# An RWKV block with routed experts: the gated rows are turned behind the k product instead of between r and k

## What is computed

```python
h = _layernorm(x, ln1_g, ln1_b)
hp = _shift(h)
xr = tm_mu_r * h + (1.0 - tm_mu_r) * hp      # xk, xv alike
r = jax.nn.sigmoid(jnp.einsum('btc,dc->btd', xr, tm_Wr))
k = jnp.einsum('btc,dc->btd', xk, tm_Wk)
v = jnp.einsum('btc,dc->btd', xv, tm_Wv)
ek = jnp.exp(tm_u + k)
wkv = ek * v / (ek + 1e-08)
x = x + jnp.einsum('btc,dc->btd', r * wkv, tm_Wout)
```

## Time and profile before

| | |
|---|---|
| median of 3 runs | 1719.45 us (1712.07 to 1720.55) |
| profiled execution, device time | 1702.0 us |
| its span in the profile | 1700.3 us |
| PE busy | 1643.6 us (97%), 8817 matmuls |
| DVE busy | 1326.2 us (78%) |
| ACT busy | 770.3 us (45%) |
| POOL busy | 417.9 us (25%) |
| mean granted clock of TensorE | 0.993 |

### The profile page before, as it was taken

How to read it: one execution, slowest core, us unless ns; L and a number is a source line. 1 busy time by engine, 2 the same in 40 slices (tenths; PEclk the granted TensorE clock), 3 DMA queues, 4 the chain that set the end, 5 groups by cost and what they waited for, 6 DMA issues and landing times.

```text
span 1700.3 us, 26873 instructions
## 1 busy us (share of the span) xinstructions
PE 1643.6 (97%) x8817; PEld 1426.7 (84%) x8817; DVE 1326.2 (78%) x2553; ACT 770.3 (45%) x1138; POOL 417.9 (25%) x505
## 2 busy tenths in 40 slices
PE   4899999999989999999999999999999999999998
PEld 1578788888768888888888888999999999998997
DVE  3999999998698788888788775777777777776872
ACT  2444434333445555454545423555555555552331
POOL 2254444343322111323232351000000000006740
PEclk9999999999999999999999999999999999999999
DMA  9622222322544443655554689788878888866861
GB/s 317 222 76 93 80 99 74 99 74 75 202 149 154 151 149 123 223 183 201 180 197 173 223 318 312 240 287 298 286 259 279 284 299 285 266 219 215 277 209 38
DMA packets 138980, 335.32 MB, mean 197 GB/s; under 512 B 20568, under 2 KB 20568, under 8 KB 133232
## 3 DMA queue, kind: packets, MB, share of 16 engines
q1 hardware_dynamic: 103904, 248.09, 43.6%
q10 hardware_dynamic: 24720, 52.21, 8.6%
q0 software_dynamic: 10240, 33.56, 5.7%
HBM read 230.21 MB, written 103.60 MB: 196 GB/s over the span
## 4 chain that ended last, share of the span: by engine, by line
PE 73%; DVE 15%; DMA 4%; issue 3%; SPq 2%; ACT 2%; POOL 1%; DVEq 0%; ACTq 0%; POOLq 0%
PE bank L701 17%; PE bank L703 17%; PE bank L702 17%; PE bank L712 5%; PE bank L2412 5%; PE bank L2410 5%; PE bank L2411 5%; PE bank L2405 2%; DVE stage L1714 2%; DVE mix L1793 1%; DVE xm_lo L1799 1%; DMA expert_in_rows<-y_rows 1%; SPq L798 1%; DMA mod_rows<-ca_rows 1%; PE bank L2394 1%
## 5 line engine op out<-in xcount | busy, mean ns | idle before, releaser
L701 PE MATMUL bank<-gu_hi,ex_x_hl 128*128 128x352 f32 x1080 | 359.9, 333 | 0.1
L703 PE MATMUL bank<-gu_hi,ex_x_hl 128*128 128x352 f32 x1080 | 348.5, 323 | 0.0
L702 PE MATMUL bank<-gu_lo,ex_x_hl 128*128 128x352 f32 x1080 | 348.4, 323 | 0.0
L1281 POOL DMA_INDIRECT raw<-expert_out_rows,out_slots x64 | 74.9, 1170 | 536.7 <-DMA expert_out_rows<-y_rows 513.0
L701 PEld LDWEIGHTS bank<-gu_hi,ex_x_hl 128*128 128x128 f32 x1080 | 203.7, 189 | 0.4 <-issue 0.3
L702 PEld LDWEIGHTS bank<-gu_lo,ex_x_hl 128*128 128x128 f32 x1080 | 204.0, 189 | 0.0
L703 PEld LDWEIGHTS bank<-gu_hi,ex_x_hl 128*128 128x128 f32 x1080 | 203.3, 188 | 0.0
L1888 DVE TENSOR_TENSOR hid<-bank,sg_t 128x352 f32<-128x352 f32 x135 | 70.2, 520 | 126.8 <-PE bank L703 107.7
L2410 PE MATMUL bank<-dn_hi,hid_hi 128*128 128x512 f32 x405 | 161.7, 399 | 3.9 <-DVE hid_lo L1892 3.9
L2412 PE MATMUL bank<-dn_hi,hid_lo 128*128 128x512 f32 x405 | 160.0, 395 | 0.0
L2411 PE MATMUL bank<-dn_lo,hid_hi 128*128 128x512 f32 x405 | 158.7, 392 | 0.0
(11 more groups left out here) (257 smaller groups left out, 3835.9 us busy)
## 6 DMA issues: line engine op xcount, KB each, us to landing
raw<-in_ex_gu SPq DMA_DIRECT2D x40, 1408.0 KB, 6.5
raw<-in_ex_dn SPq DMA_DIRECT2D x40, 512.0 KB, 4.7
ex_x<-expert_in_rows SPq DMA_DIRECT2D x71, 256.0 KB, 6.3
expert_out_rows<-y_rows ACTq DMA_DIRECT2D x71, 256.0 KB, 6.1
h_rows<-h_t SPq DMA_DIRECT2D x64, 256.0 KB, 2.6
h_turned<-h_hl ACTq DMA_DIRECT2D x32, 512.0 KB, 3.0
ex_x_hl<-h_turned ACTq DMA_DIRECT2D x32, 512.0 KB, 3.7
x_t<-in_x SPq DMA_DIRECT2D x32, 256.0 KB, 2.7
```

Of the source, the lines that this page charges most:

```text
L701: pe.matmul(acc, act_hi[i], w_hi[i], start=(i == 0), stop=False)
L702: pe.matmul(acc, act_hi[i], w_lo[i], start=False, stop=False)
L703: last = pe.matmul(acc, act_lo[i], w_hi[i], start=False, stop=(i == chunks - 1))
L1281: pool.indirect_dma_start(rows[:, pair % 2, a, :], None, ys_d, bass.IndirectOffsetOnAxis(ap=out_slots[:, k, n:n + 1], axis=0)).then_inc(ar ...
```

## The change

In PE's list of stages the pair `(trw, 2)` goes from between `(r, 0)` and `(k, 0)` to between `(k, 0)` and `(t1, -2)`. The lists of the other engines stay as they are, and so do the semaphores.

```diff
-            time_lead, time_lag, stages_of = in_turn((r, 0), (trw, 2), (k, 0), (t1, -2), (v, 0), (o, 2))
+            time_lead, time_lag, stages_of = in_turn((r, 0), (k, 0), (trw, 2), (t1, -2), (v, 0), (o, 2))
```

## The result

The changed kernel is slower by 0.3%: 1721.87 us against 1716.03 us (medians of 22 runs each), a difference of 5.8 us. The ratio over all the runs is 1.0030, with a 95% interval of 1.0019 to 1.0042; of 1716.03 us that is +5.1 us, between 3.3 and 7.2. The forecast was +4.1 us. A second comparison gave 1.0029 (1.0014 to 1.0043).

The account below looks back on a forecast made before the run. PE was taken to set the pace in the loop, a chain through ACT, POOL and DVE where time mixing ends. Pairs 0, loop 0, join 3.0, clock 1.1 sum to 4.1 us: 1723.6 us, range 1713 to 1732.

Parts of the forecast that it names:

- The loop hides the move: Steps 2 to 29: the later turn costs nothing, with 0.81 us to spare at rw_lo; step stays 12.06 us.
- the rival of a slipping loop: Loop steps: rw_hi released so late that o waits in each step; 1732 us at 0.3 us excess; chance 0.02.
- The pair of turns saves nothing: Steps 2 to 29: two turns side by side save 0.3 to 0.6 us by the trace, taken as 0.
- Step 30 makes PE late by 0.2 us: Step 30: xm_hi, xm_lo and xh go later with rw_hi, so PE's turn of xh is about 0.2 us late.
- Step 31 costs 3.0 us: Step 31, the join: late rw_hi delays the chain to the turn of xh; 3.0 us, not given back.
- The clock falls behind the pause and costs 1.1 us: Behind PE's 3.2 us pause at the join: clock falls to half for some 3.4 us, costing 1.1 us.
- the rival in which the clock stays: At the join: the stall comes without a fall of the clock; +3.0 us, 1722.5 us; chance 0.22.
- The sum: Whole kernel: pairs 0, loop 0, join 3.0 and clock 1.1 us make 4.1 us.
- The hidden join: Step 31: the delay at the join is hidden; 0 us, 1719.5 us; chance 0.08.
- the cheap pair: Loop steps: the second of two adjacent turns costs half, 6.2 us come back; 1717.3 us; chance 0.05.
- the paired turns: Loop: eight transposes without a product drop the clock; 1.7 us per fall, at most 48 us; chance 0.03.

Follow-up runs that it names:

- f4: Kernel before, but in the hardware loop the turn of the gated rows stands behind that of the normalized rows; ratio 1.0022, repeated 1.0000.
- f2: Kernel before, but in the hardware loop the turn of the gated rows stands behind v, directly in front of o; ratio 1.0234.
- e1: Changed kernel, but in step 31 the turn stands between r and k as before; ratio 1.0008, repeated 0.9999.
- e2: Kernel before with the turn moved behind k in step 31 alone; ratio 1.0019.
- e4: Changed kernel; in step 31 DVE does channel mixing's first column and mixes ahead of rw_lo, POOL their difference ahead of rw; ratio 0.9993.
- e3: Changed kernel plus 12 matmuls with unused result on PE in front of step 31's turn of xh, filling its wait; ratio 1.0034.
- after_again: The changed kernel once more, as a control, against the kernel before; ratio 1.0029.
- f1: Kernel before with step 31's DVE and POOL stages ordered as in e4; ratio 1.0012, repeated 0.9992.

## Why the prediction was right

- **The loop hides the move.** Right. `rw_lo` and `xm_lo` stayed in place and the step is 12.06 us, so the rival of a slipping loop falls; `xm_hi` moved by 0.10 us (0.26 were given, the late side). f4 shows that the cover is thicker than what the change used, f2 that it ends.
- **The pair of turns saves nothing.** Right in size, wrong in sign. The trace of before gave a saving of 0.3 to 0.6 us; there is a loss of 0.2 to 0.3 us, 0.01 us a step. That is the grain of the distances on which the estimate rested; where the 0.01 us comes from is not shown.
- **Step 30 makes PE late by 0.2 us.** Wrong, it does not: the step before the r of step 31 has 11.98 us, as before 11.99. Counted from the r of step 30, `xm_hi` and `xm_lo` start 2.65 us later, not 2.80, and `xm_lo` ran for 1.76 us instead of 2.03, so `xh` is only 2.37 us later:

```profile
427.16 1.76 DVE L1720 TENSOR_TENSOR xm_lo<-stage,xm_hi 128x1536 fp32r<-128x1536 f32 x1 [0.68 <-ACT xm_hi L1351]
```
- **Step 31 costs 3.0 us.** The mechanism was right and the term is 2.75, smaller by the 0.2 us of step 30. e1, e2 and e4 show it from three sides. One thing was overlooked: the prediction lets POOL's `diff` wait for DVE alone, and says of POOL's `rw` only that it comes later than the turn anyway. That holds in the loop; in step 31 `rw` waits for the turn and stands in front of `diff`.
- **The clock falls behind the pause and costs 1.1 us.** It fell in all three profiles with that pause (3.1 us) and cost 0.85 to 0.95 us; e3, with the pause filled, has none of it. So the rival in which the clock stays falls too.
- **The sum** was 4.1; the trace has 4.0, and the time says 3.3 to 7.2 us. That the two sums are so close is partly luck: 0.3 us too little for the pairs stands against 0.25 too much for the join and 0.15 to 0.25 too much for the clock. Whether the 1 us between 4.0 and the middle of that interval is anything stays open; e2 came out below its trace by half a microsecond.
- **The rivals.** The hidden join falls with e2, the cheap pair with the 340.9 us. The clock did not fall behind the paired turns, for the stretch from step 3 to step 31 of after_again has clock 1.00:

```profile
89.06:429.92 340.86, 338.71 (x1569) 275.26 (x1568) 318.86 (x752) 133.30 (x224) 148.58 (x164) 1.00 0.25 83
```

The rule of the Trainium skill (page "TensorE: Matmul & The Clock Gate", section "Part 4: PE-mode transpose"), that transposes don't count as busy as matmuls do, had no consequence here for 28 pairs of turns.

## What to carry to other kernels

A stage that is moved later is hidden only where the in-order queue of its consumer is still busy with earlier work, so look for the steps where that queue is shorter, here where two phases join; one step of 30 made nearly all of this cost. There, ask what stands behind each consumer, in every engine's queue, rather than when the consumer itself is needed: with the second phase's mixes and their difference put ahead, PE did not wait for the same late turn. And a new pause of PE can have a price beyond its length, when the clock falls behind it: here 0.95 us on top of 2.75. Before a long wait or fall in one profile is put down to a change, look for it in a second profile of the kernel before.

## What the runs showed that was not expected

DVE and POOL instructions last longer when they stand beside each other. In the loop POOL's `var`, one column of 128 numbers, lasts as long as it stands beside DVE's `xm_lo`; in f2, where the two are apart, both are short. POOL in the kernel before, step 13, and in f2:

```profile
221.77 1.71 POOL L1155 TENSOR_TENSOR var<-mv1h,eps 128x1 f32<-128x1 f32 x1
```
```profile
279.48 0.19 POOL L1155 TENSOR_TENSOR var<-mv1h,eps 128x1 f32<-128x1 f32 x1 [0.24 <-DVE mv1h L1693]
```

DVE's `xm_lo` is 2.42 us in the first case and 1.76 us in the second. Step 30 is alike: before, POOL's `rw` ran until 0.42 us after `xm_lo` had started, and `xm_lo` took 2.03 us; in the changed kernel `rw` ended 0.64 us ahead of it, and it took 1.76.

The closest comparison is e4 against f1, which differ only in where PE turns the gated rows. In step 31 of f1 POOL's `rw` stands beside DVE's eight mixes, in e4 it comes 1.15 us behind them. The mixes of f1's second profile, to be laid beside the 2.18 us of e4 above:

```profile
433.35 3.28 DVE L1795 SCALAR_TENSOR_TENSOR mix<-diff,vecs,h2T 128x128 f32<-128x128 f32 x8
```

The difference is in one of the eight, which lasted 1.44 us, where the others and all of e4's last 0.34 to 0.35; both profiles of f1 have it. What the two engines share is not shown.
